# Twelve fused transformer layers: centred value weights, squares on ScalarE, norms a round ahead and biases in the residual

## The reference

```
# L0_attn: causal attention, 16 heads of 128
out = einsum('bqhe,hed->bqd', softmax(q k' / sqrt(128)) v, W_O) + b_O

# L3_attn: two sublayers of a retention network, 8 heads of 32, causal decay D
for i in range(2):
    xn  = layer_norm(x, ln_gamma, ln_beta)
    q, k, v = xn @ Wq[i], xn @ Wk[i], xn @ Wv[i]
    y   = einsum('bhnm,bmhd->bnhd', (q k') * D, v)
    y   = (y - mean_head(y)) * rsqrt(var_head(y) + 1e-5) * gn_gamma[i] + gn_beta[i]
    ret = (silu(xn @ Wg[i]) * y) @ Wo[i] + x
    rn  = layer_norm(ret, ln_gamma, ln_beta)
    x   = gelu(rn @ W1[i] + b1[i]) @ W2[i] + b2[i] + ret

# L3_ffn: latent attention and a mixture of experts
h   = x + attention(rmsnorm(x, ln1_w))
out = h + moe(rmsnorm(h, ln2_w))          # 1 shared and 7 routed experts, top 2
```

## Time and profile before

| | us |
|---|---|
| median of 3 runs (lowest, highest) | 3598.69 (3598.42, 3602.27) |
| profiled execution: its own time | 3597.89 |
| its span, first to last instruction | 3596.1 |

### The profile page before, as it was taken

How to read it: one execution, slowest core, us unless ns; L and a number is a source line. 1 busy time by engine, 2 the same in 40 slices (tenths; PEclk the granted TensorE clock), 3 DMA queues, 4 the chain that set the end, 5 groups by cost and what they waited for, 6 DMA issues and landing times. The chain is left out here.

```text
span 3596.1 us, 63959 instructions
## 1 busy us (share of the span) xinstructions
PE 2895.3 (81%) x24052; PEld 2020.0 (56%) x24100; DVE 2264.0 (63%) x4833; ACT 1480.0 (41%) x3050; POOL 588.4 (16%) x934
## 2 busy tenths in 40 slices
PE   6776699977867877749996869789999978787777
PEld 3333488776645555525654335456556557666666
DVE  6999644433658888776564832367777764444754
ACT  4899511112454645344442122155555533222222
POOL 5222100000002222111110032221211211111000
PEclk8899799988977778669998978899999989889788
DMA  4999900000010000010002040000000002000000
GB/s 121 198 204 206 215 0 0 0 24 6 15 53 3 3 2 3 2 75 6 9 9 72 2 140 23 3 4 3 3 6 3 3 27 116 1 0 0 1 1 12
DMA packets 316501, 141.44 MB, mean 39 GB/s; under 512 B 296221, under 2 KB 305950, under 8 KB 312613
## 3 DMA queue, kind: packets, MB, share of 16 engines
q1 hardware_dynamic: 308072, 138.46, 16.1%
q10 hardware_dynamic: 8256, 0.52, 0.2%
HBM read 67.65 MB, written 3.15 MB: 20 GB/s over the span
## 5 line engine op out<-in xcount | busy, mean ns | idle before, releaser
L1251 ACT ACTIVATE l0x_pb<-l0x_ex,l0x_neg_max,l0x_q_scale 128x2048 uint16<-128x2048 f32 x128 | 267.1, 2088 | 36.3 <-POOL l0x_neg_max L1354 25.0
L1150 PE MATMUL l0x_s_ps<-l0x_kT,l0x_qT 128*128 128x512 bf16 x466 | 167.0, 441 | 86.3 <-DVE l0x_ex L1449 42.8
L1447 DVE TENSOR_SCALAR_CACHE_REDUCE l0x_ex<-l0x_s_ps 128x1024 f32<-128x1024 f32 x128 | 156.3, 1221 | 15.2 <-PE l0x_s_ps L1150 14.5
L1449 DVE TENSOR_SCALAR_CACHE_REDUCE l0x_ex<-l0x_s_ps 128x1024 f32<-128x1024 f32 x128 | 156.2, 1221 | 0.0
L1150 PEld LDWEIGHTS l0x_s_ps<-l0x_kT,l0x_qT 128*128 128x128 bf16 x512 | 33.9, 102 | 155.6 <-DVE l0x_ex L1449 105.1
L264 PE MATMUL l3x_bank<-l3x_w_kv_x,l3x_ctxT 128*128 128x512 f32 x256 | 117.4, 601 | 4.4 <-ACT l3x_ctx_q L765 3.7
L2229 PEld LDWEIGHTS l1a_bank<-l1a_u,l1a_gm 64*64 64x64 f32 x2048 | 95.8, 193 | 17.7 <-issue 17.1
L1160 PEld LDWEIGHTS l0x_o_ps<-l0x_v,l0x_vT 128*128 128x128 f16 x2048 | 71.4, 99 | 60.6 <-DMA l0x_vT<-l0x_pb 30.3
L2229 PE MATMUL l1a_bank<-l1a_u,l1a_gm 64*64 64x8 f32 x2048 | 98.5, 235 | 7.7 <-DVE l1a_gm L2582 7.7
L264 PE MATMUL l2f_bank<-l2f_w,l2f_ln_yT 128*128 128x352 f32 x256 | 104.3, 542 | 0.0
L2221 PE MATMUL l1a_bank<-l1a_r,l1a_r 32*64 32x64 f32 x2048 | 70.9, 278 | 40.2 <-DVE l1a_r L2563 35.1
(11 more groups left out here) (756 smaller groups left out, 7774.9 us busy)
## 6 DMA issues: line engine op xcount, KB each, us to landing
l2f_wproj_raw<-in_L_xattn_wproj SPq DMA_DIRECT2D x2, 2048.0 KB, 12.8
l3a_w<-in_L_attn_W SPq DMA_DIRECT2D x4, 1024.0 KB, 10.6
l2f_w<-in_L_ffn_w SPq DMA_DIRECT2D x1, 2816.0 KB, 11.3
l0x_ex<-in_ctxT SPq DMA_DIRECT2D x8, 256.0 KB, 4.9
l0a_wq<-in_L_attn_W_Q SPq DMA_DIRECT2D x1, 2048.0 KB
l0a_wk<-in_L_attn_W_K SPq DMA_DIRECT2D x1, 2048.0 KB
l0x_vT<-l0x_pb SPq DMA_TRANSPOSE x128, 4.7
l0a_wv<-in_L_attn_W_V SPq DMA_DIRECT2D x1, 2048.0 KB, 7.9
```

The source lines that it names most:

```text
L1150: ins = mm(s_ps[:, j * 512:(j + 1) * 512], qT[:, h, :], kT[:, h // 2, j * 512:(j + 1) * 512], start=True, stop=True)
L1251: s.activation(pb[:, h % 4, :], ex[:, h % 4, :], ACT.Exp, scale=q_scale[:, h:h + 1], bias=nb[:, h:h + 1], accum_out=sums[:, h:h + 1]).then ...
L1447: v.tensor_scalar(ex[:, h % 4, 0:1024], s_ps[:, 0:1024], 1.0, None, ALU.mult, ALU.max, accum_out=low_max[:, h:h + 1]).then_inc(o.up(scores ...
L1449: v.tensor_scalar(ex[:, h % 4, 1024:2048], s_ps[:, 1024:2048], 1.0, None, ALU.mult, ALU.max, accum_out=high_max[:, h:h + 1]).then_inc(o.up ...
```

## The change

It does five things.

1. l3_attn: at the start, DVE subtracts from each head's 32 columns of the value weights their mean (`centre`), for both sublayers. y then has no mean per head, and the mean, its scaling and the subtraction go. The square moves to ACT, which reads y from PSUM.
2. l3_attn: gamma and beta of the per-head norm are folded into the gate. POOL forms `skewed` = gate x beta and gate x gamma (two 128x256 products per tile and sublayer) behind the SiLU; DVE's second pass is y x rstd, x gate, + skewed.
3. l3_attn and l3_ffn: the two norms that stand at the head of a round are computed for round t + 1 within round t: in l3_attn behind the second sublayer's inner norm, in l3_ffn in three pieces behind the gated products of experts 1, 3 and 5 (`AHEAD`). PE's transposes and ACT's scaling of them stand at the end of the round. The two rounds are written out (`for t in range(ROUNDS)`) instead of a loop.
4. l3_attn: the bias `b2` is loaded spread over 128 partitions (256 KB, before 2 KB), POOL adds it to the residual (`biased`), and the ones matmul goes.
5. l0_attn: the same with `bo` (128 KB, before 1 KB). POOL adds it to the tile of x behind the norm (`add_bias`), one tile ahead.

```diff
@@ l0_attn @@
-                nc.tensor.matmul(y_bank, env.ones_row[:, 0:P], bo[:], start=True, stop=False)
-                project_up(nc, y_bank, lambda c: oT[:, c, :], lambda c: wo[:, c, :], H, start=False).then_inc(y_ps.sem, 1)
+                project_up(nc, y_bank, lambda c: oT[:, c, :], lambda c: wo[:, c, :], H).then_inc(y_ps.sem, 1)
...
+            def add_bias(t):
+                pool.wait_ge(norm.normed.sem, norm.normed.value(t))
+                xt = tile_of(env.x, t)
+                nc.gpsimd.tensor_tensor(xt, xt, bo[:], ALU.add).then_inc(x_biased.sem, 1)
...
             with pool.Fori(0, TILES - 1) as t:
                 o = Order(pool, L.order["pool"], t)
                 o.t = t + 2
                 whole(norm.pool(o))
+                add_bias(t + 1)
...
                 dve.wait_ge(y_ps.sem, y_ps.value(t))
+                dve.wait_ge(x_biased.sem, x_biased.value(t))
@@ l3_attn, PE @@
+                    pe.wait_ge(v_centred, l + 1)
...
-                    nc.tensor.matmul(dve_bank[:, 0:D], env.ones_row[:, 0:P], b2[:, l * D:(l + 1) * D], start=True, stop=False)
-                    project(nc, dve_bank[:, 0:D], lambda c: hid[:, c, :], lambda c: w2[:, l, c, :], FC, start=False).then_inc(ffn_ps.sem, 1)
+                    project(nc, dve_bank[:, 0:D], lambda c: hid[:, c, :], lambda c: w2[:, l, c, :], FC).then_inc(ffn_ps.sem, 1)
+                if t + 1 < ROUNDS:
+                    yield from first.tensor(pe, t + 1, act_bank)
@@ l3_attn, ACT @@
-                    s.activation(sg[:], act_bank[:, 0:D], ACT.Silu).then_inc(o.up(g_ready), 1)
+                    s.activation(sg[:], act_bank[:, 0:D], ACT.Silu).then_inc(o.up(gate_squared), 1)
+                    yield
+                    act.wait_ge(y_ps.sem, y_ps.value(t, k))
+                    s.activation(sq[:], dve_bank[:, 0:D], ACT.Square).then_inc(o.up(gate_squared), 1)
@@ l3_attn, POOL @@
+                    yield from steps(3)
+                    pool.wait_ge(gate_squared.sem, gate_squared.value(t, 2 * l + 1))
+                    g.tensor_tensor(skewed[:], sg[:], gn_b[:, l, :], ALU.mult).then_inc(o.up(), 1)
+                    pool.wait_ge(o.sem, o.at())
+                    g.tensor_tensor(sg[:], sg[:], gn_g[:, l, :], ALU.mult).then_inc(o.up(gate_rstd_bias), 1)
+                    pool.wait_ge(gate_rstd_bias.sem, o.at(gate_rstd_bias))
+                    yield
+                    pool.wait_ge(have_var.sem, have_var.value(t, k))
+                    g.tensor_tensor(rstd[:], var[:], env.neg_half[:].broadcast_to([P, H]), ALU.pow).then_inc(o.up(gate_rstd_bias), 1)
...
+                    g.tensor_tensor(biased[:], ret[:], b2[:, l, :], ALU.add).then_inc(o.up(gate_rstd_bias), 1)
@@ l3_attn, DVE @@
+            def centre(o, l):
+                v, heads = nc.vector, w["v"][:, l].rearrange("p c (h e) -> p (c h) e", e=HD)
+                o.eng.wait_ge(*((second_loaded, 16 * 7) if l else (first_loaded, 16 * 5)))
+                v.reduce_sum(v_mean[:, l, :], heads, AX_X).then_inc(o.up(), 1)
+                o.eng.wait_ge(o.sem, o.at())
+                v.scalar_tensor_tensor(out=heads, in0=v_mean[:, l, :].unsqueeze(2).broadcast_to([P, DC * H, HD]), scalar=-1.0 / HD, in1=heads, op0=ALU.mult, op1=ALU.add).then_inc(v_centred, 1)
...
-                    v.reduce_sum(mean[:], dve_bank[:, 0:D].rearrange("p (h e) -> p h e", e=HD), AX_X).then_inc(o.up(), 1)
-                    v.tensor_scalar(mean[:], mean[:], 1.0 / HD, None, ALU.mult).then_inc(o.up(), 1)
-                    v.tensor_tensor(by_head(y), dve_bank[:, 0:D].rearrange("p (h e) -> p h e", e=HD), wide(mean), ALU.subtract).then_inc(o.up(), 1)
-                    v.tensor_tensor(sq[:], y[:], y[:], ALU.mult).then_inc(o.up(), 1)
+                    dve.wait_ge(gate_squared.sem, gate_squared.value(t, 2 * l + 2))
...
-                    v.tensor_tensor(by_head(y), by_head(y), wide(rstd), ALU.mult).then_inc(o.up(), 1)
+                    v.tensor_tensor(by_head(y), dve_bank[:, 0:D].rearrange("p (h e) -> p h e", e=HD), wide(rstd), ALU.mult).then_inc(o.up(), 1)
-                    v.tensor_tensor(y[:], y[:], gn_g[:, l, :], ALU.mult).then_inc(o.up(), 1)
+                    v.tensor_tensor(y[:], y[:], sg[:], ALU.mult).then_inc(o.up(), 1)
-                    v.tensor_tensor(y[:], y[:], gn_b[:, l, :], ALU.add).then_inc(o.up(), 1)
-                    v.tensor_tensor(y[:], y[:], sg[:], ALU.mult).then_inc(o.up(yg_ready), 1)
+                    v.tensor_tensor(y[:], y[:], skewed[:], ALU.add).then_inc(o.up(yg_ready), 1)
...
+                    if l == LAYERS_ - 1 and t + 1 < ROUNDS:
+                        o.t = t + 1
+                        yield from norm.vector(o, tile_of(env.x, (t + 1) * WAYS + i))
+                        yield from first.vector(o, norm.y[:])
+                        o.t = t
@@ l3_ffn, DVE, behind the gated product of expert i @@
+                    if t + 1 < ROUNDS and i in AHEAD:
+                        o.t = t + 1
+                        if i == AHEAD[0]:
+                            normalising = norm.vector(o, tile_of(env.x, (t + 1) * WAYS + n))
+                            next(normalising)
+                        if i == AHEAD[1]:
+                            whole(normalising)
+                            normalising = first_rms.vector(o, norm.y[:])
+                            next(normalising)
+                        if i == AHEAD[2]:
+                            whole(normalising)
+                        o.t = t
@@ l3_ffn, PE @@
                 add_expert(NE - 1).then_inc(y_ps.sem, 1)
+                if t + 1 < ROUNDS:
+                    yield from first_rms.tensor(pe, t + 1, other)
@@ both, every engine @@
-            with pe.Fori(0, TILES // WAYS) as t:
+            in_turn(*(tile["tensor_ahead"](pe, 0) for tile in tiles))
+            for t in range(ROUNDS):
                 in_turn(*(tile["tensor"](pe, t) for tile in tiles))
```

More of the change, by code:

```diff
@@ L1643, in _ @@
                 whole(norm.pool(ahead))
+            pool.wait_ge(env.own.sem, env.own.value())
+            add_bias(0)
             with pool.Fori(0, TILES - 1) as t:
@@ L4234, in _ @@
             s = nc.scalar
-            with act.Fori(0, TILES // WAYS) as t:
+            in_turn(*(tile["scalar_ahead"](act) for tile in tiles))
+            for t in range(ROUNDS):
                 in_turn(*(tile["scalar"](act, t) for tile in tiles))
@@ L4239, in _ @@
         def _(pool):
-            with pool.Fori(0, TILES // WAYS) as t:
+            in_turn(*(tile["gpsimd_ahead"](pool) for tile in tiles))
+            for t in range(ROUNDS):
                 in_turn(*(tile["gpsimd"](pool, t) for tile in tiles))
@@ L4245, in _ @@
             v = nc.vector
-            with dve.Fori(0, TILES // WAYS) as t:
+            in_turn(*(tile["vector_ahead"](dve) for tile in tiles))
+            for t in range(ROUNDS):
                 in_turn(*(tile["vector"](dve, t) for tile in tiles))
@@ L4406, in scalar_program @@
                 yield from steps(2)
-                yield from rms.scalar(o, other, scale=ln2_w, k=2)
+                yield from rms.scalar(o, other, scale=ln2_w)
                 yield
@@ L4417, in scalar_program @@
                     s.activation(hidT[:], other[:, 2 * I:3 * I], ACT.Copy).then_inc(o.up(hidT_ready), 1)
+                if t + 1 < ROUNDS:
+                    o.t = t + 1
+                    yield from first_rms.scalar(o, other, scale=ln1_w)
+                    o.t = t
                 yield
@@ L4493, in vector_program @@
                 dve.wait_ge(o.sem, o.at())
[L4494 removed]
+                yield from rms.vector(o, h[:])
                 yield
@@ L4528, in _ @@
             pe.wait_ge(block_set.sem, block_set.value())
-            with pe.Fori(0, TILES // WAYS) as t:
+            in_turn(*(tile["tensor_ahead"](pe) for tile in tiles))
+            for t in range(ROUNDS):
                 in_turn(*(tile["tensor"](pe, t) for tile in tiles))
```

221 lines of the change are left out of this document (142 added, 79 removed).

## The result

The changed kernel takes 3548.72 us (median of 4 runs, 3545.95 to 3552.13) against 3600.35 for the kernel before on the same chip: ratio 0.9861, 95% interval 0.9845 to 0.9877. Forecast: 3556, range 3546 to 3567, faster. The profiled execution has a span of 3543.8 us against 3596.1, so 52.3 us less where the sum had 42.7. A second execution of the same kernel, profiled later, has 3549.4. Two questions follow: which terms were mis-sized, and what differs between two executions of one program.

A forecast was written before the change was run, and what follows sets the result against it. PE was taken as the engine the others wait for, with known holes, in all three changed layers. Terms summed to -42.7 us, from 3597.9 to 3555.2, or 3555.9 against the median: forecast 3556 us, range 3546 to 3567.

The forecast's parts named there:

- Bias matmuls: l3_attn and l0_attn: dropping the one-row bias matmuls saves 0.62 and 0.63 us per tile, -9.9 and -5.0 us.
- the sign I named: l3_attn feed-forward: no bias matmul rows left and a period of 3.65 us per tile.
- Turn of l3_attn: Between l3_attn's rounds: PE's hole goes, -13.4 us; first q, k, v no longer slowed by the clock, -0.8 us.
- Turn of l3_ffn: Between l3_ffn's rounds: hole -12.0, slower work behind it -1.0; one late transpose behind expert 3, +1.8; net -11.2 us.
- Per-head norm: l3_attn's four retention sites: shorter DVE passes, POOL's products and powers on the path, -1.1 us each, -4.4 us.
- Start of l3_attn: First q matmul waits for later weights and DVE's centring: +2.0 us (0 to +2.5).
- table loads: Rival: Square in l3_attn and Exp in l3_ffn need ScalarE table loads on the path, 7.7 us, 3564; chance 0.07.
- POOL as the wait: Rival, per-head norm: dearer products and slowed powers make each site +0.3 instead of -1.1 us, 3562; chance 0.10.
- Code starvation: Rival, written-out rounds of l3_attn and l3_ffn: new code stalls, 13 of them (45 us) give 3601; chance 0.02.
- The rival of the clock: Rival, l3_attn output projections: shorter hole leaves the clock up, 4 x 1.9 = 7.6 us more saved, 3548; chance 0.08.

The follow-up runs named there:

- the three edits: Changed kernel with the centred-weights wait behind q and k, beta's product on DVE, and l3_ffn's next-round norms in four pieces behind experts 1, 3, 4, 6: 3544.18 us.

## Why the prediction was right, and where its terms were off

The sign, the range and each mechanism held; the sum was 9.6 us short of the first profile. That the measured 3548.7 lies inside the range, 7 us under the forecast, is in part luck: the low end of 3546 was set by a rival that did not happen (the clock staying up in the projections), and the room went for the larger part to a bias matmul that cost more than I had put down, which no bound covered. Term by term, forecast and measured in that profile:

- *Bias matmuls:* -9.9 and -5.0; measured 4 x 3.28 = -13.1 (from the end of the first feed-forward matmul to that of the second, 17.10 to 13.82) and 8 x 0.82 = -6.6. The mis-sized step is "0.62 us per tile": the distance from the start of the bias matmul to the next. It left out what the one-row matmul adds to its neighbours, and so the sign I named, a period of 3.65 us per tile, came out at 3.45. This is 4.8 us, the largest single miss, and it stood in the trace: from one L4095 to the next (the earlier trace rows show the first) it is 4.27 us, where 16 passes of 0.216 need 3.45.
- *Turn of l3_attn:* -13.4 and -0.8; measured -14.05 from the last W2 matmul to q, and q, k, v 11.58 to 10.84, -0.74. The transposes behind a hole were slower too, which I had priced for q, k and v only.
- *Turn of l3_ffn:* -13.0 and +1.8; measured 19.27 to 5.74 from the last expert's transpose to the head matmuls, -13.5, and one transpose 1.48 late, +1.45. (The +1.8 had a slip of 0.1: 1.55 and 0.35 make 1.90 per tile, not 1.94.)
- *Per-head norm:* -4.4; measured 4 x -0.96 = -3.8. POOL's products took 0.72, not 0.65. With the power taken away it showed that POOL's chain is the path.
- *Start of l3_attn:* +2.0; measured +2.0, and +2.6 in the second pair of executions.
- *The rest*, -3.5 in this profile: no term of mine. In l0_attn -1.3: the last projection, at full clock, takes 1.7 us less. Why the kernel before drops there and the changed one does not is not settled: putting the bias matmul back did not bring it. In l3_attn -1.1, and +5.6 in the second pair of executions (that of the changed kernel against that of before), where the changed kernel's output projections and first feed-forward matmuls are 5.3 us the longer ones. In l3_ffn -1.2, not parted further.

The terms of the sum, as measured, come to -48.4, and the two executions stand at -52.3 and, against the second of before (3597.3), -47.9. Of the rivals, table loads cost nothing: 14 on ScalarE in these two layers against 16, none at Square, and the two new ones at Exp end 5.5 us before it is released (the first in the rows below). POOL as the wait came with the sum's price, not its own. Code starvation did not: no DVE stall at either turn. The rival of the clock gave 3548, the number that was measured, but it isn't what happened: a hole shortened by a tenth left the projections at 21.0 and 25.3 us against 22.4. Its mechanism and price are real all the same, and filling the hole collects 6.5 us or more.

Timeline of ScalarE at the first Exp of l3_ffn, changed kernel:

```profile
3315.40 1.28 ACT L4504 ACT_TABLE_LOAD   x1
3322.23 1.06 ACT L4504 ACTIVATE l3f_e<-l3f_e 128x1024 f32<-128x1024 f32 x1 [5.55 <-DVE l3f_e L4601]
```

## What to carry to other kernels

Price a matmul by the period of the stream with it against the stream without it, not by the distance to its next: an operand with one row cost 0.82 us where 128 rows of the same product cost 0.43. A gain of a few microseconds in a layer where the clock falls in holes can't be counted from one pair of profiles: two executions of one program were 7.2 us apart in this one. Count it at its own place, take the kernel's time from medians, and profile the unedited kernel twice; or fill the holes first, then count. Work moved under another engine's run came free here where piece and old work together stayed within the pace there (1.9 us against a pace of 1.29 made one transpose late; under 1.3 none).

## What the runs showed of the hardware

- One program, two executions: 7.2 us apart in a layer of 335 us, and the difference lies in projections, first feed-forward matmuls, q, k and v (127.2 against 134.9 us), with a lower mean granted clock (0.56 against 0.75 in the projection shown). Single runs of the changed kernel spread by 6 us (3545.95 to 3552.13). So one pair of profiles doesn't settle a term under 7 us in such a layer, unless it is read at work that no hole precedes.
- Matmuls that nobody reads, in holes of 1 to 4 us, made a kernel faster by 0.25% with nothing else changed (before, filled) and by 0.3% on top of the change. The fastest kernels of this study, fillers with the three edits, stand at 0.982 of before.
- The one-row operand: 0.31 us from pass to pass at each change of the row count against 0.216.
- POOL, two operands of 128x256: 0.72 us alone, 0.91 beside a DVE operation with two SBUF operands; a power of 128x8 took 1.64 beside such operations in the changed kernel.
